# Scattering 480 unprojected columns per tile in the second layer's edge loop

## The reference

```python
w = jax.nn.relu(edge_feature @ W_fc1) @ W_fc2          # 64 -> 64 -> 224
w0, w1, w2, w3, w4 = jnp.split(w, [64, 128, 160, 192], axis=-1)
xs, xv = s[dst], v[dst]
out0a = w0 * xs
out0b = w3 * (jnp.einsum('emi,ei->em', xv, sh1) * INV_SQRT3)
out1a = (w1 * xs)[:, :, None] * sh1[:, None, :]
out1b = w2[:, :, None] * xv
out1c = w4[:, :, None] * (jnp.cross(xv, sh1[:, None, :]) * INV_SQRT2)
tp = concatenate([out0a, out0b, out1a, out1b, out1c])  # 96 scalars, 3 x 128
agg = segment_sum(tp, src, num_segments=N) / DENOM
out_s = agg[:, :96] @ W_out_s + skip_s
out_v = einsum('nmi,mk->nki', agg_v, W_out_v) + skip_v
```

## Time and profile before

| | |
|---|---|
| median of 3 runs | 13,953.6 us |
| the profiled execution | 13,971.6 us |
| its span, first to last instruction | 13,969.8 us |
| TensorE busy (matmul) | 10,808 us, 77% |
| VectorE busy | 8,552 us, 61% |
| GpSimd busy | 8,206 us, 59% |
| ScalarE busy | 4,566 us, 33% |
| mean granted TensorE clock | 0.747 |
| moved by DMA | 1,138 MB |

### The profile page before, as it was taken

The page is one execution under the profiler, slowest core; times in us unless marked ns, Lnnn a source line. Parts: engine busy times, 40 slices in busy tenths (PEclk is TensorE's granted clock), DMA queues, the critical chain, the costliest instruction groups (busy, mean ns, idle before and its releaser), DMA issues. The chain is left out here.

```text
span 13969.8 us, 239951 instructions
## 1 busy us (share of the span) xinstructions
PE 10808.1 (77%) x55109; PEld 9201.4 (66%) x55109; DVE 8552.1 (61%) x21245; ACT 4566.3 (33%) x11584; POOL 8205.8 (59%) x8212
## 2 busy tenths in 40 slices
PE   2988888856658999999999457777777656788885
PEld 2888888845556777777777456666666645555564
DVE  4677777789634444444444467777777796566663
ACT  1444444430122222222222235555555501233331
POOL 4777777748625555555655255555555375566660
PEclk7777777768756666666666678888888787788995
DMA  3443444437403333333333322222222274233321
GB/s 91 92 91 91 91 92 92 92 104 207 118 14 65 62 62 63 61 63 61 64 61 61 96 66 67 69 69 69 69 68 68 58 191 128 70 82 82 83 81 45
DMA packets 1350653, 1138.02 MB, mean 81 GB/s; under 512 B 558798, under 2 KB 1147331, under 8 KB 1349895
## 3 DMA queue, kind: packets, MB, share of 16 engines
q0 software_dynamic: 347904, 478.51, 18.0%
q1 hardware_dynamic: 854716, 549.77, 14.3%
q10 hardware_dynamic: 147914, 108.40, 3.0%
HBM read 767.61 MB, written 368.33 MB: 81 GB/s over the span
## 5 line engine op out<-in xcount | busy, mean ns | idle before, releaser
L738 POOL DMA_INDIRECT e_gs<-tab_src,e_ix x1568 | 1680.4, 1072 | 1264.9 <-DVE e_msg L2095 801.6
L677 PE MATMUL e_psF<-w_ident,e_F 128*128 128x128 f32 x6272 | 1395.9, 335 | 756.3 <-ACT e_F L1983 504.7
L738 POOL DMA_INDIRECT e_gd<-tab_dst,e_ix x1568 | 1667.6, 1064 | 477.8 <-issue 473.5
L789 POOL DMA_INDIRECT acc<-e_sums,e_row x784 | 1249.9, 1594 | 1183.5 <-ACT e_sums L1687 1044.4
L677 PEld LDWEIGHTS e_psF<-w_ident,e_F 128*128 128x128 f32 x6272 | 950.8, 180 | 928.6 <-issue 882.3
L707 ACT ACTIVATE e_FT<-e_psF 128x384 f32<-128x384 f32 (+1 forms) x2352 | 1067.6, 454 | 914.2 <-PE e_psF L677 569.4
L1801 POOL DMA_INDIRECT e_g<-tab_src,e_er x976 | 993.3, 1018 | 609.9 <-DVE e_rows L1897 322.0
L1627 PEld LDWEIGHTS e_psS<-e_same,e_rows 128*128 128x128 f32 x6272 | 1129.9, 275 | 313.6 <-issue 310.7
L1627 PE MATMUL e_psS<-e_same,e_rows 128*128 128x128 f32 x6272 | 1248.0, 371 | 1.2 <-DVE e_same L763 1.2
L713 ACT ACTIVATE e_O<-e_psO 128x352 f32<-128x352 f32 (+1 forms) x1568 | 688.1, 439 | 961.7 <-PE e_psO L660 271.7
L1563 PE MATMUL s_psS<-s_wv,s_hot 128*128 128x168 f32 (+1 forms) x3904 | 669.7, 315 | 412.6 <-POOL s_wv L1521 213.7
(11 more groups left out here) (492 smaller groups left out, 27261.0 us busy)
## 6 DMA issues: line engine op xcount, KB each, us to landing
val<-e_O SPq DMA_DIRECT2D x392, 320.0 KB
s_val<-val ACTq DMA_DIRECT2D x244, 320.0 KB, 3.3
s_val<-val SPq DMA_DIRECT2D x244, 320.0 KB
e_krow<-in_src_t SPq DMA_DIRECT2D x196, 256.0 KB
sums<-e_total SPq DMA_DIRECT2D x244, 192.0 KB
e_es<-in_es SPq DMA_DIRECT2D x196, 130.0 KB
e_gs<-tab_src,e_ix POOLq DMA_INDIRECT x1568
e_gd<-tab_dst,e_ix POOLq DMA_INDIRECT x1568
```

The lines of the kernel that those rows point to most:

```text
L677: last = nc.tensor.transpose(psF[:, P * g:P * g + P], F[:, k, P * g:P * g + P], ident[:, :])
L738: pool.indirect_dma_start(into[t][u][:, k, :], None, tables[t], bass.IndirectOffsetOnAxis(ix[u][:, t, k:k + 1], 0))\
L789: pool.indirect_dma_start(acc[k], bass.IndirectOffsetOnAxis(T["row"][u][:, k:k + 1], 0), T["sums"][u][:, k, :], None, compute_op=ALU.add). ...
```

## The change

The edge loop no longer projects. A tile's sums are now one product per tile, with `same` stationary and the 480 columns of `rows` moving (`pe_sums`), copied to SBUF by ScalarE (`act_sums`) and scattered as they are. `rows` has 480 columns without a pad. The accumulators have 480 columns, in clearing too. The node phase adds up four accumulators of 480 columns, turns the totals and the state (stages `turn_s`, `turn_v`, `turn_x`) and multiplies by output and skip weights into the same PSUM sums (`product`, `product_v`). The next pass's loads are issued after `move_v` instead of after `whole`. The gate becomes 0.5 + 0.5 tanh, and the output weights lose the factor 1/2 that they had for it.

```diff
-ACC_W = (168, 192, 164, 384)
+ACC_W = (168, 480, 164, 384)
...
+def pe_sums(nc, pe, i, u, T, values, psS, S, ready):
+    passed = S.sem("pe_passed")
+    wait_apart(pe, S.sem("same"), i + 1, passed)
+    wait_apart(pe, *ready, passed)
+    for k in range(TM):
+        wait_apart(pe, S.sem("sums"), i * TM + k - len(psS) + 1, passed)
+        nc.tensor.matmul(psS[(k) % len(psS)], T["same"][u][:, k, :], values[:, k, :], start=True, stop=True)\
+            .then_inc(S.sem("summed"), 1)
+
+def act_sums(nc, act, i, u, j, T, psS, S):
+    for k in range(TM):
+        wait(act, S.sem(f"added{k}"), (i - 1) * 16)
+        act.wait_ge(S.sem("summed"), i * TM + k + 1)
+        nc.scalar.activation(T["sums"][u][:, k, :], psS[k % len(psS)], ACT.Copy).then_inc(S.sem("sums"), 1)
...
-    wn, width, out = 224, 4 * P, C0 + C1 + C1V
+    wn, width = 224, 96 + 3 * 128
...
-                for c in range(4):
-                    last = nc.tensor.matmul(psS[:, k % 2, P * c:P * c + P], rows[u][:, k, P * c:P * c + P], T["same"][u][:, k, :],
-                                            start=True, stop=True, skip_group_check=True)
...
-                nc.tensor.matmul(o[:, 0:96], f[0:96, 0:P], W["l1_out_s"][:, :], start=True, stop=True, skip_group_check=True)
-                for d in range(3):
-                    last = nc.tensor.matmul(o[:, 96 + C1 * d:96 + C1 * d + C1], f[:, P * d + P:P * d + 2 * P], W["l1_out_v"][:, :],
-                                            start=True, stop=True, skip_group_check=True)
...
-                    sums(i, u, 0)
-                    for k in range(1, TM):
-                        sums(i, u, k)
-                        project(i, k - 1)
+                    pe_sums(nc, pe, i, u, T, rows[u], banks, S, (sem("products"), i + 1))
...
-        stages += ["copy", "turn_x", "move_x", "product", "pair", "sum", "joined"] if post == 1 else ["pair"]
+        stages += ["pair", "sum"] if post == 1 else ["pair"]
...
-        if post == 3:
+        if post in (1, 3):
             stages += ["turn_s", "move_s", "turn_v", "move_v", "turn_x", "move_x", "product", "product_v"]
...
-    used = {None: None, 0: "turn_a", 1: "whole", 2: "turn_a", 3: "move_v"}[post]
+    used = None if post is None else "turn_a" if post in (0, 2) else "move_v"
...
+                            times(B.wideB, 0, (B.aT[:, :], W["l1_out_s"][:, :]), (B.sT[0:64, :], W["l1_skip_s"][:, :])).then_inc(B.done, 1)
...
+                            for t in range(G):
+                                c = slice(P * t, P * t + P)
+                                nc.tensor.matmul(B.wideA[:, t, 0:C1V], B.vT[:, c], W["l1_skip_v"][:, :], start=True, stop=False, skip_group_check=True)
+                                for d in range(3):
+                                    last = nc.tensor.matmul(B.wideA[:, t, C1 * d:C1 * d + C1], B.gT[d][:, c], W["l1_out_v"][:, :], start=False,
+                                                            stop=True, skip_group_check=True)
...
+                        if post == 1:
+                            tt(B.ag[0][:, :, :], B.ag[0][:, :, :], B.ag[1][:, :, :], ALU.add)
+                            tt(B.ag[2][:, :, :], B.ag[2][:, :, :], B.ag[3][:, :, :], ALU.add)
                         nc.vector.tensor_copy(B.res[:, :, :], X(B, j)).then_inc(B.done, 1)
...
-                            last = stt(out=B.out[:, :, C0 + C1 * d:C0 + C1 * d + C1], in0=B.th[:, :, :], scalar=1.0,
-                                       in1=B.ag[0][:, :, 96 + C1 * d:96 + C1 * d + C1], op0=ALU.add, op1=ALU.mult)
+                        tt(comp(B.out[:, :, C0:CX]), comp(B.wideA[:, :, 0:C1V]), bcast(B.th[:, :, :], 2, 3), ALU.mult).then_inc(B.done, 1)
```

More of the change, by code:

```diff
@@ L1585, in cross_convolution @@
         rows = [S.sb(f"rows{u}", [P, TM, width]) for u in range(2)]
-        turned = [S.sb(f"turned{u}", [P, width]) for u in range(2)]
-        psH, psS, psP = S.ps("psH", [64, 512]), S.ps("psS", [P, 2, 512]), S.ps("psP", [P, 512])
+        psH, psS = S.ps("psH", [64, 512]), S.ps("psS", [P, 2, 512])
         psWs = [S.ps(f"psW{u}", [P, TM, 256]) for u in range(2)]
+        banks = [psS[:, k, 0:width] for k in range(2)]
         sem = S.sem
@@ L1676, in body @@
                 if m := i_of(2):
[L1677 to L1682, removed]
-                    def result(k):
-                        wait(act, sem(f"added{k}"), (i - 1) * 16)
-                        act.wait_ge(sem("projected"), i * TM + k + 1)
-                        nc.scalar.activation(T["sums"][u][:, k, :], psP[:, 0:out], ACT.Copy).then_inc(sem("sums"), 1)
-                    move(0)
[L1690 to L1693, removed]
+                    act_sums(nc, act, *m, T, banks, S)
             steps(act, NM, LAST, body)
@@ L1698, in _ @@
         def _(dve):
-            for R in rows:
-                nc.vector.memset(R[:, :, 96:P], 0.0).then_inc(sem("padded"), 1)
             dve_dirs(dve)
@@ L2168, in __init__ @@
             self.th = sb("th", [P, G, C1])
+        if post in (1, 3):
+            self.gT = [sb(f"gT{d}", [P if post == 1 else 96, G * P]) for d in range(3)]
+            self.aT = sb("aT", [96, G * P])
         if post == 3:
-            self.gT = [sb(f"gT{d}", [96, G * P]) for d in range(3)]
-            self.aT = sb("aT", [96, G * P])
             self.ang, self.whole_t = sb("ang", [P, 2, G]), sb("whole_t", [P, 2, G])
@@ L2207, in node_phase @@
         if post == 1:
-            stages += ["silu", "gate_t", "gated", "whole"]
+            stages += ["silu", "gate_t", "gate_half", "gated", "whole"]
         if post == 2:
@@ L2445, in _ @@
                         move(B.fvTb, B.psB, 64).then_inc(B.done, 1)
-                if post == 3:
+                if post in (1, 3):
+                    per = 128 if post == 1 else 96
                     for B in both:
@@ L2538, in _ @@
             with dve.Fori(0, PAIRS) as j:
[L2539 to L2542 removed]
+                if post is not None:
                     for B in both:
                         at(dve, "pair", B, j)
[L2545 to L2557 removed]
+                        dve.wait_ge(B.loaded, (j + 1) * 16 * (TM if post == 1 else G))
+                        if post == 1:
+                            tt(B.ag[0][:, :, :], B.ag[0][:, :, :], B.ag[1][:, :, :], ALU.add)
+                            tt(B.ag[2][:, :, :], B.ag[2][:, :, :], B.ag[3][:, :, :], ALU.add)
                         nc.vector.tensor_copy(B.res[:, :, :], X(B, j)).then_inc(B.done, 1)
+                    if post == 1:
+                        for B in both:
+                            at(dve, "sum", B, j)
+                            tt(B.ag[0][:, :, :], B.ag[0][:, :, :], B.ag[2][:, :, :], ALU.add).then_inc(B.done, 1)
                 if post in (0, 2):
@@ L2616, in _ @@
                     for B in both:
+                        at(dve, "gate_half", B, j)
+                        ts(B.th[:, :, :], B.th[:, :, :], 0.5, 0.5, ALU.mult, ALU.add).then_inc(B.done, 1)
+                    for B in both:
                         at(dve, "gated", B, j)
-                        for d in range(3):
-                            last = stt(out=B.out[:, :, C0 + C1 * d:C0 + C1 * d + C1], in0=B.th[:, :, :], scalar=1.0,
-                                       in1=B.ag[0][:, :, 96 + C1 * d:96 + C1 * d + C1], op0=ALU.add, op1=ALU.mult)
-                        last.then_inc(B.done, 1)
+                        tt(comp(B.out[:, :, C0:CX]), comp(B.wideA[:, :, 0:C1V]), bcast(B.th[:, :, :], 2, 3), ALU.mult).then_inc(B.done, 1)
                     for B in both:
```

97 lines of the change are left out of this document (33 added, 64 removed).

## The result

On the first chip the changed kernel takes 13,199.98 us (median of 4 runs, 13,194.85 to 13,225.13) against 13,959.93 (4 runs, 13,917.46 to 13,992.57): ratio 0.946, 95% interval 0.943 to 0.949. The prediction was made from the first chip's profile, and I read that one first.

The account below looks back on a forecast made before the run. TensorE, 91% busy at mean clock 0.64, was taken to bound the second layer's edge loop. 13,971.6 us minus 894 (loop) plus 166 (node phase) gave 13,244, stated as 13,240; range 13,110 to 13,600.

Parts of the forecast that it names:

- Loop period 13.3 us: Second layer's edge loop: GpSimd's eight DMAs sum to 13.06 us a macro, plus 2% waits; down from 17.86, gain 894.
- its low-clock sum of 12.7 us: TensorE in the changed edge loop, per macro: hidden layer 1.97, weights 3.35, four 480-column products 7.4 us.
- DMA engines 8.6 to 12.4 us a macro: Edge loop transfers: scatters 5.8 to 9.7 us at 182 to 303 ns a row, plus gathers and fixed loads; no cost.
- Scatter on GpSimd 1.59 us: Edge loop: GpSimd's issue of a scatter stays 1.59 us with 1,920-byte rows; cost by bytes would be 3.98 us.
- Node phase +166 us: Second layer's node phase: seven passes +150 us in all, plus later first load; range +130 to +230 us.
- turns and products, 24.4 us: Each node pass: turned totals, turned x and 48 products per pair of groups, priced from the last node phase.
- Front sums: Start of each node pass: four pair sums of 2.2 us, two copies and the first `sum`, 11.6 us together.
- the first load: Node phase: only the first pass's 7.86 MB load is seen, costing some 17 us more; later ones are hidden.
- Clearing at nothing: First layer's edges: clearing accumulators writes 33.6 MB more, hidden beside a 2,601 us loop; at most 112 us uncovered.
- rival 4: Edge loop: a chain of latencies holds 17.5 us a macro and the node phase is paid; 14,070 us, chance 0.05.
- Rivals 2 to 4: Edge loop: 2, DMA engines bound, 13,580 us, chance 0.12; 3, scatter issue grows with row, 15,070, 0.06; 4, 14,070, 0.05.
- Rival 1: Edge loop: TensorE stays the bound at low clock, 14.0 to 14.5 us a macro; 13,380 to 13,480 us, chance 0.17.

Follow-up runs that it names:

- b1: The kernel before, unchanged, traced on a high-clock chip (one where it takes some 11,740 us): 11,743.9 us.
- b2: The changed kernel, unchanged, against the kernel before on one high-clock chip: 11,912.4 us against 11,738.1, ratio 1.015.

## Why the prediction was right, and where it wasn't

On the chip whose profile it was made from, 13,240 us against 13,200 measured, within 13,110 to 13,600 and on the side that had 0.89. By its terms:

- **Loop period 13.3 us: 12.96.** The sum 13.06 was right to 0.1 (gathers average 1.050 us, not 1.073); the 2% of other waits that I allowed didn't come. Gain 956, not 894. That TensorE would leave the path was right, and its low-clock sum of 12.7 us too high, since all but the 480-column products ran at high clock, and part of these too.
- **DMA engines 8.6 to 12.4 us a macro: 7.8 for scatters, 10.7 in all (82.3% of 12.96).** The bounds 182 and 303 ns a row held.
- **Scatter on GpSimd 1.59 us: 1.593.** Shown from 768 to 3,072 bytes.
- **Node phase +166 us: +201.** The term that was mis-sized most is turns and products, 24.4 us "at mixed clock", which measured 32.4: from 7,053 to 7,072 us of the pass read, with the vector products (1.38 us for six, 13.6 us in all), the granted clock was 0.50, in a phase whose mean is 0.60. Front sums (11.4 for 11.6) were right. Two smaller errors went the other way: the old pass that the prediction read took 41.4 us where the mean is 42.8, and the first load, taken at 17 us, has some 10. The price "all products at low clock" had been kept in the range's upper end, and should have been the estimate: the phase before the change had 0.62.
- **Clearing at nothing:** the first layer's edges took 2,974.2 - 378.3 = 2,595.9 us, against 2,601.3. Right.

The errors, 62 us too little gain, 35 too little cost, and 13 us elsewhere, leave 40. That they cancel in part is luck.

**What the prediction missed** is that its largest term rests on a granted clock that isn't the kernel's own. It took 0.64 in the loop before as given. On a high-clock chip the same loop has 0.81 and nothing to give, and the change is slower by 1.5%: timed there, the forecast would have had the wrong sign, in a way that none of the four rivals names: rival 4 (the loop isn't freed, the node phase is paid) is the nearest in its sum, but by a chain of latencies, where here the old loop was at GpSimd's period already. The hint stood in the profile of before: TensorE at 91% busy and mostly low clock in one stage, with 486 ns for a 384-column pass at high clock showing what the same work could cost. A line "if the clock were high, the old loop would be GpSimd's too, 13.0 us, and the change +166" could have been computed from those rows, as a rival with its own price.

**Rivals 2 to 4** fell on the first chip by the DMA share of 0.82, the 1.593 us of a scatter and the period of 12.96 us. **Rival 1** (TensorE stays bound at low clock) had the Trainium skill's rule beside it (TensorE: Matmul & The Clock Gate, "Part 1": a busy array gets 2.4 GHz, an idling one 1.2). It did not come true on the first chip. In the rule's favour: with doubled sums the clock was higher in both kernels (0.89 for 0.76; 0.87 on a low-clock chip, where the first chip gave the loop 0.64). Against it as a full account: with less work the changed kernel's clock was 0.76, higher than the 0.64 of the busier loop before. Open is why a low-clock chip leaves the loop of the kernel before at 0.64, and why it differs between chips; the runs show the fact alone.

## What to carry to other kernels

When a stage's bound is TensorE at low clock, work out the next bound and the same stage at high clock: the change is worth the difference to that bound only where the clock is low. Work moved from a loop into a serial phase was paid on both kinds of chip (here 200 us), while the gain depended on the chip (956 or 4 us). An indirect scatter of 128 rows cost GpSimd 1.59 to 1.63 us from 768 to 3,072 bytes a row, so it is paid by the instruction, not by the bytes; longer rows were free up to a DMA share of 0.93, the highest tried.

## What the runs showed that I had not expected

- The same kernel takes 11,740 us on some chips and 13,960 to 14,260 on others. Only part of it is the second layer's loop (12.96 against 17.86 us a macro, 955 us): the third layer's edges take 2,222.7 us in b1 against 2,984.8, and the first layer's 2,421.8 against 2,601.3, with granted clock 0.78 against 0.75 there. The third layer's edges have 0.94 where the first chip's trace has 0.83 (kernel before, then b1; columns as in rows 1), and the last convolution 1.00 for 0.89. The granted clock is higher in each of these stages; how much of the gap outside the second layer it makes was not worked out.

```profile
8120.00:11060.00 2940.00, 2175.23 (x12893) 1980.84 (x12893) 2149.73 (x4724) 1542.63 (x4717) 1694.50 (x1539) 0.83 0.27 68
```

```profile
7000.00:9150.00 2150.00, 1832.33 (x12718) 1674.00 (x12717) 2087.12 (x4651) 1470.25 (x4660) 1666.29 (x1510) 0.94 0.36 92
```

- More work on TensorE made a kernel faster: doubling the turned sums took 222 us off 14,258 (one execution against nine), with the loop at 0.87 of full clock.
- An accumulating row's time on the DMA engines is not a line in its bytes: 122, 244 and 284 ns for 768, 1,920 and 3,072 bytes.
- At one and the same period and on one chip the clock was higher with more work: 0.76 with 8.4 busy us of TensorE a macro in b2, 0.89 with 10.6 in the doubled sums.
